# Mixing the first eight blocks of activations by row halves, and two wide warming matmuls for seven narrow ones

## The reference, cut to what matters

```python
def _L0_cond_ref(x, condition, weights):      # x (64, 32, 512), weights (16, 32, 32)
    W = weights[condition]
    return jnp.einsum('bct,bcd->bdt', x, W)
...
x = x + _L0_attn_ref(_L0_cond_ref(x, itok_B_0_15, L0_cond_weights), Wq, bq, Wk, bk, Wv, bv, Wo, bo, gq, gk)
x = x + _L0_ffn_ref(_L0_cond2_ref(x, ...), ...)
```

## Time and profile before

| | |
|---|---|
| median of 3 runs | 1451.25 us (1451.07 to 1451.78) |
| the profiled execution, its own time | 1450.27 us |
| its span, first to last instruction | 1448.4 us |
| PE busy | 1443.8 us (100%) |
| DVE, POOL, ACT busy | 1079.1, 746.3, 726.7 us |
| mixing matmuls of the two chunks (L666, from qk) | 64 records, 7.4 us |
| warming matmuls (L645) | 18 records, 4.1 us |

### The profile page before, as it was taken

How to read it: one execution, slowest core, us unless ns; L and a number is a source line. 1 busy time by engine, 2 the same in 40 slices (tenths; PEclk the granted TensorE clock), 3 DMA queues, 4 the chain that set the end, 5 groups by cost and what they waited for, 6 DMA issues and landing times.

```text
span 1448.4 us, 34721 instructions
## 1 busy us (share of the span) xinstructions
PE 1443.8 (100%) x14507; PEld 1200.6 (83%) x14507; DVE 1079.1 (75%) x1507; ACT 726.7 (50%) x1331; POOL 746.3 (52%) x530
## 2 busy tenths in 40 slices
PE   9999999999999999999999999999999999999999
PEld 8788888888888888888888888888888888888887
DVE  8788868687786777875478888867987667667663
ACT  7766676766766667676333333334432322222221
POOL 7668777777777877776345555514561111112100
PEclk9999999999999999999999999999999999999999
DMA  4211011110111011102443343447653334244230
GB/s 152 66 45 45 31 38 45 45 44 25 45 45 45 29 39 45 45 31 67 138 155 137 131 136 134 145 151 244 200 195 110 103 118 132 85 136 132 74 118 30
DMA packets 106989, 135.13 MB, mean 93 GB/s; under 512 B 6224, under 2 KB 89424, under 8 KB 106320
## 3 DMA queue, kind: packets, MB, share of 16 engines
q1 hardware_dynamic: 105968, 132.49, 27.7%
q10 hardware_dynamic: 864, 0.42, 0.1%
HBM read 86.75 MB, written 46.14 MB: 92 GB/s over the span
## 4 chain that ended last, share of the span: by engine, by line
PE 97%; DVE 1%; ACT 1%; DMA 0%; issue 0%; SPq 0%; DVEq 0%
PE bank L717 42%; PE bank L960 25%; PE bank L736 21%; PE bank L919 4%; PE bank L845 3%; PE bank L988 1%; PE bank L1006 1%; DMA qk<-in_x_nat 0%; PE bank L666 0%; DVE qreg L1708 0%; PE bank L1017 0%; PE bank L974 0%; ACT xs_hi L1160 0%; DVE wa L1624 0%; DVE sqst L1708 0%
## 5 line engine op out<-in xcount | busy, mean ns | idle before, releaser
L717 PE MATMUL bank<-xs_hi,wa 128*128 128x512 f32 x1792 | 563.3, 392 | 0.1
L1527 POOL TENSOR_TENSOR accr<-accr,sqst 128x512 f32<-128x512 f32 x248 | 353.2, 1435 | 147.7 <-ACT sqst L1197 107.5
L717 PEld LDWEIGHTS bank<-xs_hi,wa 128*128 128x128 f32 x1792 | 336.3, 188 | 74.1 <-DVE qk L1775 2.3
L717 PE MATMUL bank<-xs_lo,wa 128*128 128x512 f32 x896 | 348.7, 389 | 0.0
L960 PE MATMUL bank<-ot,wo_main 128*128 128x512 f32 x1344 | 316.4, 392 | 0.0
L960 PEld LDWEIGHTS bank<-ot,wo_main 128*128 128x128 f32 x1344 | 249.5, 188 | 52.6
L736 PE MATMUL bank<-wv,xs_hi 128*128 128x512 f32 (+1 forms) x1008 | 282.6, 366 | 0.1
L1624 DVE TENSOR_TENSOR wa<-wraw,wa 128x256 fp32r<-128x256 f32 (+1 forms) x160 | 157.0, 982 | 96.7 <-ACT wa L1106 95.0
L1322 ACT ACTIVATE ot<-bank,vec 128x256 fp32r<-128x256 f32 x256 | 100.3, 476 | 239.0 <-PE bank L960 146.6
L736 PEld LDWEIGHTS bank<-wv,xs_hi 128*128 128x128 f32 x1008 | 182.1, 189 | 32.9 <-issue 1.9
L717 PEld LDWEIGHTS bank<-xs_lo,wa 128*128 128x128 f32 x896 | 168.3, 188 | 33.2
(11 more groups left out here) (224 smaller groups left out, 1726.9 us busy)
## 6 DMA issues: line engine op xcount, KB each, us to landing
values_b<-v_spill SPq DMA_DIRECT2D x60, 512.0 KB, 4.9
wraw<-in_wqk SPq DMA_DIRECT2D x32, 512.0 KB, 3.5
v_spill<-qk SPq DMA_DIRECT2D x64, 256.0 KB, 2.3
v_spill<-sqst SPq DMA_DIRECT2D x64, 256.0 KB, 2.2
score_spill<-sqst SPq DMA_DIRECT2D x32, 256.0 KB, 2.0
wraw<-in_wv SPq DMA_DIRECT2D x16, 512.0 KB, 5.1
wraw<-score_spill SPq DMA_DIRECT2D x16, 512.0 KB, 4.0
spare<-in_wo SPq DMA_DIRECT2D x15, 512.0 KB, 4.8
```

Of the source, the lines that this page charges most:

```text
L717: ins = pe.matmul(dst[:, :], wa[:, col:col + P], xpart[:, j - 1, kt, n * CH:(n + 1) * CH], start=(first and k == 0), stop=(k == 5), skip_g ...
L1527: pool.tensor_tensor(a, a, sq_slot(count), ALU.add).then_inc(acc_done, 1)
```

## The change

The seven warming matmuls of 128 moving columns at the start become two of 512 moving columns (the same 128 ones, read four times). The two behind the small matmuls stay.

In both chunks each matmul of a block is cut in two. Since a mixing matrix is block diagonal, token rows 0 to 63 reach only output columns 0 to 63, and rows 64 to 127 only columns 64 to 127. `mix_rows(0, ...)` multiplies the upper 64 rows, `mix_rows(1, ...)` the lower ones, each with 64 moving columns and still 128 stationary columns. A chunk is walked in six steps k = 0 to 5: in step k the upper rows of block k and the lower rows of block k - 2, alternating tile by tile where both exist, so two steps have the upper rows alone, two have both, and two the lower alone. The lower rows of a block wait, by the new semaphore `mix_upper`, until its upper rows are done; `mixed` is raised after the lower rows. The eight blocks of `mix_group` are as before.

```diff
             pe.wait_ge(warm_ready, 1)
-            warm_up(7)
+            for _ in range(2):
+                pe.matmul(bank[7][:, :].rearrange("p (a n) -> p a n", a=4), rqk[:, 0:P],
+                          rqk[:, 0:P].unsqueeze(1).broadcast_to([P, 4, P]), start=True, stop=True)
...
+            def mix_rows(half, block, t):
+
+                g, r, c, i = block
+                rows = slice(half * 64, (half + 1) * 64)
+                return pe.matmul(mix_bank(g, r)[:, t * P + half * 64:t * P + (half + 1) * 64],
+                                 x_in[c][rows, t, i * P:(i + 1) * P], mixw[rows, c * TC + t, rows], start=True, stop=True)
+
             def mix_chunk(c):
 
                 pe.wait_ge(ld_x[c], 16)
                 pe.wait_ge(mix_first if c == 0 else mix_done, NB)
-                for i in range(KI):
-                    mix_block_of(i % 2, (0, 3)[i // 2] if c == 0 else (1, 2)[i // 2], c, i)
+                blocks = [(i % 2, (0, 3)[i // 2] if c == 0 else (1, 2)[i // 2], c, i) for i in range(KI)]
+                for k in range(KI + 2):
+                    upper, lower = k < KI, k >= 2
+                    if lower:
+                        pe.wait_ge(mix_upper, (KI if c else 0) + k - 1)
+                    for t in range(TC):
+                        if upper:
+                            up = mix_rows(0, blocks[k], t)
+                        if lower:
+                            low = mix_rows(1, blocks[k - 2], t)
+                    if upper:
+                        up.then_inc(mix_upper, 1)
+                    if lower:
+                        low.then_inc(mixed, 1)
```

More of the change, by code:

```diff
@@ L336, in build @@
         mixed = sem("mixed")
+        mix_upper = sem("mix_upper")
         x_act = sem("x_act")
```

## The result

The changed kernel takes 1459.59 us, the median of six runs (1454.70 to 1463.79); the kernel before took 1451.32 us beside it (1451.07 to 1451.78). The ratio is 1.0055, 95% interval 1.0043 to 1.0068: 8.3 us slower. The direction was predicted, the size was not: 1459.59 lies above the range of 1450.8 to 1455.5.

The account below looks back on a forecast made before the run. PE, busy for 1443.8 of 1448.4 us, was taken to bound the kernel. Mixing +3.58, warming +0.1 and given back -0.3 made +3.4 us, from a median of 1451.25 to 1454.6 us; range 1450.8 to 1455.5.

Parts of the forecast that it names:

- The pace of a half matmul: Mixing at the start: loading 128 stationary columns sets 0.112 us a record, 0.896 us a step, lone or double.
- The rival that a lone half goes by streaming: Mixing: streaming alone paces a lone half, 0.059 us a record; about 0.15 us less, 1451.1 us; chance 0.15.
- That halves take turns: Double steps of the mixing: row halves run in turn, 1.79 us a step, total 1458.2 us; chance 0.06.
- The size of the stage: Mixing of two chunks: 12 steps at 0.896 us, 10.75 us against 7.17 us, +3.58 us on PE.
- Given back: PE's stops in the first 38 us and DVE's low part: -0.3 us, bounds 0 and -0.8.
- Warming: Warming matmuls ahead of the mixing: wider ones delay the mixing, partly covered by the wait for x; +0.1 us.
- The clock: Rival for the mixing stage: granted clock falls to 1.2 GHz, remaining half 5 us more, about 1459 us; chance 0.07.
- the granted clock full throughout: Sign of being right in the changed profile: no fall of the granted clock anywhere.
- the pace of 0.21 us behind 6 us: Sign of being wrong: records 0.21 us apart anywhere behind 6 us.
- Behind the start nothing gives slack back: a microsecond added here is a microsecond at the end: Whole kernel after the start: PE's list has no slack, so a delay at the start counts in full.

Follow-up runs that it names:

- e9: Kernel before with each mixing matmul of the first eight blocks cut in two by moving columns, all 128 rows, 32 tiny matmuls more: 1458.13 us, ratio 1.0047.
- e8: The change with all 128 moving columns in each half matmul, lower rows added to the upper ones: 1454.79 us, ratio 1.0031.
- e4: The change with each half matmul cut again into two of 64 stationary columns (64 by 64 tiles): 1457.50 us, ratio 1.0043.
- e7: The change with 37 more tiny matmuls, so 256 instructions longer than the kernel before: 1454.44 us, ratio 1.0042.
- e1: The change's half matmuls alone, with seven narrow warming matmuls as in the kernel before: 1462.27 us, ratio 1.0072.
- e3: The change with its two chunks as one pipeline of ten steps instead of two of six: 1454.08 us, ratio 1.0023.
- e2: Kernel before with only the two wide warming matmuls, whole-row mixing, 20 instructions shorter: 1454.85 us, ratio 1.0030.
- e5: Kernel before with the two wide warming matmuls and five more tiny matmuls, restoring the instruction count: 1450.62 us, ratio 1.0000.
- e6: Kernel before with 27 more tiny matmuls, 108 instructions longer like the change, no halves or wide warming: 1452.00 us, ratio 1.0009.
- e12: Kernel before with five tiny matmuls fewer, 20 instructions shorter, no wide warming or halves: 1455.05 us, ratio 1.0026.
- e11: Kernel before with 64 by 64 tiles by halves in the first chunk only, wide warming, 21 tiny matmuls more: 1455.89 us, ratio 1.0028.

## Why the prediction was wrong

**The pace of a half matmul: right.** Lone records stand 0.112 us apart, double steps go in pairs at that pace, as predicted from the earlier trace rows. e9 shows it with all rows and half the moving columns, e8 with half the rows and all moving columns, e4 shows that the pace halves with the stationary columns. The rival that a lone half goes by streaming is refuted. The Trainium skill's page "TensorEngine Tiling (Array Packing)", section "Theoretical Speedup", gives up to twice the speed for a dimension of 64 or less. The double steps agree, with two half matmuls in the 0.112 us of one; the lone steps show that a half without its partner is no quicker than a whole. That halves take turns is refuted as well, and so is a limit by the number of instructions, since double steps issue twice as many in the same time.

**The size of the stage: a term mis-sized, by 0.6 us.** The prediction had 10.75 us and +3.58. At full clock e7 needs 10.13 us up to the first product, +2.96. Its record starts say why: between the four lone steps in the middle eight records run in pairs, where the upper rows of chunk 2 begin beside the last lower ones of chunk 0. Given back was 0.1 to 0.2 us (e7 is 4.0 us late at the first product, 3.8 at the hundredth), where the prediction had 0.3. Warming: 0.07 us later at the mixing (6.90 for 6.83), where it had 0.1.

**The clock: the step that failed.** The prediction says: "Against it: the mean loads behind the start, in L845 and L919 too, are those of the full clock, though their groups are short." From that it gave the fall 0.07, put no term for it into the sum and expected "the granted clock full throughout". But L845 works on all 128 rows and L919 on four tiles of 64 by 64 side by side, so they say nothing of one half of the rows alone. The fall was the likeliest case: five of six runs of the changed kernel have it. The prediction's price for it (5 us, 1459) was near: the median lies 4.9 us above the run at full clock. In the profiled run 6.8 us at half clock cost 1.86 us before the first product (18.89 - 6.90 = 11.99 us against e7's 10.13) and 1.3 us over the first twelve records of L739; some 2.7 us of it are left at the hundredth product, and this run is 2.8 us above the one at full clock. The place was less well named: the fall followed the sixteen matmuls in a row here, but came ahead of them in e1, and e3 has no such row. Of the signs of being wrong, the pace of 0.21 us behind 6 us is the one that came.

That the halves bring the fall is shown by e1, which differs from the kernel before in them alone: three of its four runs have it, against none of 62 of the kernel before and none of the 34 of e2, e5, e6 and e12. That a stage just as long with whole rows keeps the clock rests on e9's four runs, and these have 32 tiny matmuls more; with 37 more, e7 fell in only two of five. That the half-width moving side has a part in it rests on e8's one run in eight against the change's five in six, at another start and perhaps on another chip. So the shares are rough, and what in the halves brings the clock down is open, as is why it falls in one run and not in the next. The Trainium skill's page "TensorE: Matmul & The Clock Gate", section "HAM oscillation — how this bites in real kernels", tells of a fall after PE has stood idle; in the change and in e1 PE was busy without a gap when it fell, in e4 it stood.

**"Behind the start nothing gives slack back: a microsecond added here is a microsecond at the end": incomplete.** It left out that an edit moves all code behind it. The 108 added instructions brought a stop of PE at 694.84 us: 0.7 us of idle time in the changed kernel, 0.6 us net of what comes back 4 us later, 1.0 us of idle time in e6 without any half matmul, none in e7. A position 20 instructions lower costs 4 us. Nothing in the prediction had this; the earlier trace rows gives the count of instructions, and the instruction queue in the trace of before shows a transfer that starts at 402.4 us, one microsecond behind the end of the burst in which e2 and e12 have their first stop: the kernel before missed that stop narrowly.

**The sum as measured:** mixing 2.96 less 0.2 given back and 0.07 for the start, 2.8 us; the late stop, 0.6 in the one trace; the clock, 4.9 at the median; together 8.3, as measured. The run at full clock is 1454.70, within 0.1 us of the predicted 1454.6, but partly by luck: the stage was 0.6 us shorter, and a stop that the prediction didn't know of took its place. That the sum closes to a tenth is chance too: the trace of the change grows by another 1.2 us against that of before (7.3 less 5.5 less 0.6). Of this 0.3 us is a wait for ACT near 118 us, which every traced kernel but the one before has; 0.9 us stays unassigned, and other padded kernels show 0.2 to 1.3 us of such drift against that one trace of before.

## What to carry to other kernels

Where a small float32 matmul is paced by its weight load, as here, fewer rows or moving columns gained nothing (e7, e9); only fewer stationary columns shortened it (e4), and then code must be there in time. Compare variants at equal code length (a few tiny matmuls as padding, some 25 ns each here) before blaming an edit for a microsecond that turns up far behind it. And price half-array stretches at both levels of the clock, taking the spread of several runs with each run's granted clock for evidence, not one trace.

## What the runs showed of the hardware that was not expected

- **Code arrives in pieces of 16 KB**, and the stops fit 256 instructions a piece: the late stop is there at 108 and 364 instructions more than before (five kernels), and gone at 0 and 256 more. From the start of the transfer to PE's resuming it took 2.9 us (e2), 2.6 (e4), 2.4 (e11, from 9.34 to 11.73) and 2.4 in the changed kernel (from 692.47 to 694.84); that PE waited for just this transfer is inferred from the times. The stops were 0.4 to 3.3 us long, most of them in bursts of small matmuls.
- **The granted clock can fall while PE is busy without a gap**: at 14.94 us in the changed kernel, at 9.66 us in e1. It came back at 21.77 and 26.72 us, after the first product matmuls, which have all rows and 512 columns, had run at half clock.
- **The two row halves of the array overlap across unrelated matmuls**, without a stop at the change from lone to double steps: 0.056 us per record in pairs against 0.112 alone (e7).
